# Graph attention on one core: comparison constants read from SBUF instead of PSUM, and self loops added by 8-column products

## The reference, cut to what matters

```
scores = einsum('ehd,ehd->eh', ft[src], ft[dst]) / sqrt(13)
agg    = segment_sum(ft[src] * softmax_over_dst(scores), dst)     # attention
...
s = concatenate([src, arange(n)]);  d = concatenate([dst, arange(n)])   # self loops
out = segment_sum(h[s] * norm[:, None], d)                         # each convolution
```

## Time and profile before

| what | value |
|---|---|
| median of 3 runs | 3872.35 us (3868.58 to 3874.59) |
| profiled execution, its own time | 3876.97 us |
| its span in the profile | 3875.2 us |
| busy share of the span: PE, DVE, ACT, POOL | 91%, 60%, 46%, 61% |
| mean granted clock of TensorE | 0.901 |

### The profile page before, as it was taken

One profiled execution on the slowest core, in us unless ns is written; L12 is line 12 of the kernel. 1 busy time (PEld: TensorE's weight loads), 2 busy tenths in 40 slices (PEclk: granted clock), 3 DMA queues, 4 the chain that ended last, 5 costly groups with the idle time before them and its releaser, 6 DMA issues. The chain is left out here.

```text
span 3875.2 us, 60488 instructions
## 1 busy us (share of the span) xinstructions
PE 3542.1 (91%) x21012; PEld 2105.9 (54%) x21012; DVE 2341.8 (60%) x3454; ACT 1786.6 (46%) x4890; POOL 2357.4 (61%) x2508
## 2 busy tenths in 40 slices
PE   5799999999999999999875888999999999999999
PEld 4566666666666666666654554444544454445444
DVE  8798888888888888888743674222322242214222
ACT  4788888878778878888621464000200020002000
POOL 2577777777777777777774001775277437734772
PEclk7688888888888888888876898999999999999999
DMA  6443334334343343333323215887788678868885
GB/s 203 123 109 105 106 103 107 106 104 106 106 107 103 107 106 103 107 107 107 99 64 78 49 35 163 257 256 223 220 258 256 203 238 258 257 193 261 261 261 176
DMA packets 494657, 599.82 MB, mean 155 GB/s; under 512 B 59929, under 2 KB 426868, under 8 KB 494094
## 3 DMA queue, kind: packets, MB, share of 16 engines
q1 hardware_dynamic: 358950, 341.00, 29.2%
q0 software_dynamic: 79888, 166.31, 17.6%
q10 hardware_dynamic: 55544, 89.04, 6.6%
HBM read 488.04 MB, written 109.69 MB: 154 GB/s over the span
## 5 line engine op out<-in xcount | busy, mean ns | idle before, releaser
L923 POOL DMA_INDIRECT fts<-ft_tab,src_all x1568 | 1481.1, 945 | 477.6 <-issue 477.3
L2296 PE MATMUL cv_acc<-cv_cnt,cv_parts 128*128 128x512 bf16 (+1 forms) x6468 | 1304.7, 364 | 1.0 <-DVE cv_y L2130 1.0
L2296 PEld LDWEIGHTS cv_acc<-cv_cnt,cv_parts 128*128 128x128 bf16 x6468 | 608.3, 98 | 693.4 <-DVE cv_y L2130 1.8
L2069 POOL DMA_INDIRECT cv_slots<-hs_tab,slot_idx x600 | 568.4, 947 | 416.4 <-issue 374.0
L960 DVE TENSOR_TENSOR ohk<-iota_ps,key_cols 128x784 bf16<-128x784 f32 x720 | 665.7, 966 | 5.6
L1212 PE MATMUL agg_ps<-terms,oh 128*64 128x141 f32 x2744 | 544.9, 372 | 35.9 <-DVE terms L997 35.3
L1053 ACT ACTIVATE dist_l<-lo_iota,low 128x128 bf16<-128x128 f16 x1800 | 545.2, 387 | 17.1 <-ACT low L1048 0.7
L1212 PEld LDWEIGHTS agg_ps<-terms,oh 128*64 128x64 f32 x2744 | 472.1, 185 | 90.8 <-DVE terms L997 76.3
L1105 ACT CAST strip<-adj_ps 128x392 bf16<-128x392 f32 x720 | 341.8, 475 | 256.2 <-PE adj_ps L1156 230.1
L974 DVE TENSOR_TENSOR prod<-ftd_ps,fts 128x780 f32<-128x780 f32 (+1 forms) x392 | 271.1, 692 | 285.3 <-DMA fts<-ft_tab,src_all 275.8
L2069 POOL DMA_INDIRECT spare<-hs_tab,slot_idx x296 | 280.2, 947 | 187.4 <-issue 187.4
(11 more groups left out here) (287 smaller groups left out, 3349.8 us busy)
## 6 DMA issues: line engine op xcount, KB each, us to landing
cv_cnt<-adj SPq DMA_DIRECT2D x88, 2048.0 KB, 8.5
cv_cnt<-adj SPq DMA_DIRECT2D x44, 2176.0 KB, 9.6
adj<-strip ACTq DMA_DIRECT2D x180, 392.0 KB
fts<-ft_tab,src_all POOLq DMA_INDIRECT x1568
win<-ft_tab SPq DMA_DIRECT2D x196, 65.0 KB
hs_tab<-cv_hs ACTq DMA_DIRECT2D x24, 448.0 KB, 3.8
cv_slots<-hs_tab,slot_idx POOLq DMA_INDIRECT x600
agg_tab<-res SPq DMA_DIRECT2D x196, 35.2 KB
```

The lines of the kernel that those rows point to most:

```text
L923: nc.gpsimd.indirect_dma_start(fts[u][:, k, :], None, ft_tab[:, :], bass.IndirectOffsetOnAxis(src_all[:, n, k:k + 1], 0)).then_inc(gathere ...
L2069: nc.gpsimd.indirect_dma_start(slots[n % RING][:, e, :], None, hs_tab[:, :], bass.IndirectOffsetOnAxis(slot_idx[:, k, at:at + 1], 0)).then ...
L2296: last = nc.tensor.matmul(a[:, 0:width], parts[:, r, b, :], cnt[q][:, 0:width // SUB, (b - b0) * SUB:(b - b0 + 1) * SUB], start=(b == 0 an ...
```

## The change

It has two parts. The first takes the iota bank away: `iota_ps` and the copy that filled it are gone, and lines 955 and 960 read both inputs, iota and keys, from SBUF. The second takes `own` and `own_low` away, with their two memsets and two copies and the semaphore `own_made` that TensorE waited on once at the start. Each quarter's first count product now opens the bank, and the self loops come last: one product of 8 columns, with the identity `ident_bf` (128 x 128, bf16) as weights and 8 of its columns as the moving operand, written to the 8 places of the quarter (2 of `a`, 4 of `d`) that are the strip's own nodes. The number of one-hot instructions, of gathers and of count products is the same as before.

```
-        own = sb("own", [SUB, NA, 2 * KEYS], BF16, c)
-        own_low = sb("own_low", [SUB, 2 * P - SUB], BF16, c)
-        iota_ps = pb("iota_ps", [P, 512], F32, c)
-        own_made = sem("own_made")
...
-            nc.vector.memset(own[:], 0.0).then_inc(own_made, 1)
-            nc.vector.memset(own_low[:], 0.0).then_inc(own_made, 1)
-            dve.wait_ge(own_made, 2)
-            nc.vector.tensor_copy(own[:, :, KEYS:KEYS + HALF], ident_bf[0:SUB, 0:SUB].rearrange("p (a d) -> p a d", d=HALF)
-                                  ).then_inc(own_made, 1)
-            nc.vector.tensor_copy(own_low[:, P - SUB:P], ident_bf[0:SUB, 0:SUB]).then_inc(own_made, 1)
...
             dve.wait_ge(iotas, 1)
-            nc.vector.tensor_copy(iota_ps[:, 0:KEYS + P], iota_sb[:]).then_inc(consts, 1)
-            dve.wait_ge(consts, 8)
-            key_no, lo_no = iota_ps[:, 0:KEYS], iota_ps[:, KEYS:KEYS + P]
+            dve.wait_ge(consts, 7)
+            key_no, lo_no = iota_sb[:, 0:KEYS], iota_sb[:, KEYS:KEYS + P]
...
-                tile_of = own[:, q * QS:(q + 1) * QS, KEYS - HALF * k.j:2 * KEYS - HALF * k.j]
-                nc.tensor.matmul(adj_ps[q % 2][:, 0:QS * KEYS], own_low[:, P - SUB - SUB * k.u:2 * P - SUB - SUB * k.u], tile_of, start=True, stop=False)
+                counts_ps = adj_ps[q % 2][:, 0:QS * KEYS]
                 for a in range(QS):
                     for m in range(SC):
                         n = q * QC + a * SC + m
-                        last = nc.tensor.matmul(adj_ps[q % 2][:, a * KEYS:(a + 1) * KEYS], ohl[:, k.s, n, :],
-                                                ohk[:, k.s, n, :], start=False, stop=(a == QS - 1 and m == SC - 1))
+                        nc.tensor.matmul(counts_ps[:, a * KEYS:(a + 1) * KEYS], ohl[:, k.s, n, :], ohk[:, k.s, n, :],
+                                         start=(a == 0 and m == 0), stop=False)
+                first = SUB * k.u + q * QS * HALF
+                last = nc.tensor.matmul(counts_ps.rearrange("p (a t d) -> p a t d", a=QS, d=HALF)[:, :, k.j, :], ident_bf[:],
+                                        ident_bf[:, first:first + QS * HALF].rearrange("p (a d) -> p a d", d=HALF),
+                                        start=False, stop=True)
                 last.then_inc(adj_done, 1)
...
             zero = Group(0)
-            pe.wait_ge(own_made, 4)
             nearness(zero)
```

## The result

The changed kernel takes 4075.99 us (median of 4 runs, 4065.62 to 4082.38) against 3873.47 (3868.58 to 3877.05) for the kernel before: a ratio of 1.0521, with an interval of 1.0496 to 1.0546. It is slower by 202.5 us, where +121 was predicted; the time lies inside the range, near its upper end.

The account below looks back on a forecast made before the run. The prediction took POOL's back-to-back gathers to bound the attention; 3877.0 us profiled plus 121 of gather waits made 3998, and the median lying 4.6 lower gave 3993 us, range 3918 to 4086.

Parts of the forecast that it names:

- What bounds the kernel: Attention: POOL issues gathers back to back, one every 1.249 us; 1568 of them make 1959 us, half the kernel.
- A gather waits at its start: Attention gathers: length is 0.94 us plus what was left of a VectorE instruction with two SBUF inputs, minus 0.12.
- rival 2: Attention: gathers are not held up, VectorE gives way within its idle time; time stays at 3872 us, chance 0.08.
- 0.74 x 0.49 + 0.26 x 1.19: Attention: short-kind and long-kind waits weighted by their shares before the change, 0.67 us a group, +121 us over 180 groups.
- long kind: Groups whose `prod` starts about 3.30 us after the eighth gather's start; fourth, seventh, eighth gathers wait, together 1.19 us.
- More than 0.1 us ahead: Attention: a gather waits only if the VectorE instruction with two SBUF inputs began more than 0.1 us before it.
- short kind: Groups whose `prod` starts about 2.60 us after the eighth gather's start; only the eighth gather waits, 0.49 us.
- Rival 1: Attention: a waiting gather cannot get in between gapless VectorE instructions; 1.87 us a group, +336, about 4208 us, chance 0.07.
- Rival 3: Whole kernel: the change frees time, by a few us of setup or quicker `ohk`; some 3865 us, chance 0.02.
- `ohk` at 975 ns: VectorE in the attention: 975 ns with both inputs in SBUF against 966 before, covered by idle time, so costing nothing.
- Self loops, clock, setup: TensorE some 0.7 us less a group beside the gathers, a lower clock, fewer setup instructions: none changes the time.

Follow-up runs that it names:

- the first experiment: Against the kernel before, only the iotas moved to SBUF, self loops left as they were: 4079.4 us, 1.0533 times the kernel before.
- the third: Against the kernel before, iotas read from SBUF, but each group's 22 keys first copied by VectorE into PSUM: 3872.2 us, 1.0003 times the kernel before.

## Why the prediction was right in kind and short in size

*What bounds the kernel*: right. The gaps stayed at 477.7 us, and the gathers' 197.8 us are 99% of what the span grew by.

*A gather waits at its start for a VectorE instruction with both inputs in SBUF, and goes on 0.12 us before its end*: right, taken from two gathers of another stage, and confirmed by the first experiment against the third, which differ in where the keys lie (and in the two small copies and waits that this takes). The Trainium skill, page "SBUF — State Buffer", section "Who interferes with whom", infers that `tensor_tensor` does not stall the making of descriptors. Taken for the whole gather, as in rival 2, the measurement decides against that, with 535 of 1568 delayed and 202.5 us; these gathers also read their indices from SBUF, and which of their steps is held no run here shows.

*The weights, "0.74 x 0.49 + 0.26 x 1.19"*: this is the step that mis-sized the sum. The shares of the two kinds were read from the kernel before and taken as fixed. They hang on the length of a group: it moves the last gather's end past the strip's store, so that 146 of 160 groups become long, a share of 0.91 and not 0.26. The long kind's walk, 1.19 us a group, would have given +214; measured are 11.09 - 9.99 = 1.10 us and +202.5. The range reached the measured time only because it took in this bound, and not as the likeliest. How near the walk comes is in part luck: the fourth, seventh and eighth gather wait 0.19, 0.33 and 0.47 us in the mean where it had 0.47, 0.21 and 0.51, and the other places add 0.11, which it had at nothing. That the store sets the kinds is shown by the two runs that move it; why a store delays the landing is not.

*"More than 0.1 us ahead"*: wrong for the fourth `ohk`, which has no wait in front of it. In the kernel after it cost a wait of 12 gathers only, since the long kind's third gather comes before `most`. But it makes the short kind's walk wrong: with the third gather held, the group takes 11.57 us (the store moved), 1.58 more than before and not 0.49. Had the shares stayed as they were, the sum would have been too low even so. With the wait in front of `ohk`, the short kind's eighth waits 0.5 us, as its walk said, and the seventh 0.1, which the walk had free.

*Rival 1*: out. A waiting gather gets in between `ohl` and `ohk` and between two `ohk`, as the 1.27 and the 1.47 show. *Rival 2*: out; `ohk` took 965 ns and the gathers gave way. *Rival 3*: out; the time rose.

*`ohk` at 975 ns*: 965, so the place of the iota makes no difference to VectorE, and the line through the earlier trace rows was 10 ns high. *Self loops, clock, setup*: nothing, as predicted; the run with the self loops alone has the lower clock and the time of before.

What stays open: why an instruction two places ahead of `ohk` (`most`, with a memset between) still counts. That instructions without a wait are handed on ahead of their start, and hold gathers from then on, fits all that was seen around the fourth `ohk`, the wait that releases the gathers above all; the handing itself is not in the trace. It does not fit the run of `ohl` and three `ohk` as it stands: the first `ohk` there has no wait in front either, and yet ten gathers that started in the last 0.14 us of `ohl`, up to 0.06 us ahead of that `ohk`, took 0.94 to 0.96 us. So the reach back has been seen behind `most` alone, and not behind another instruction with both inputs in SBUF.

## What to carry to other kernels

Before moving an operand from PSUM to SBUF, look at what GpSimd does in that stretch: where it issues indirect DMAs back to back, each VectorE instruction with both inputs in SBUF, if long like `ohl` and `ohk` here, can hold one of them up for about its own length, though it takes no longer itself. Weights that are counted in the kernel before (so many groups of one kind, so many of the other) are themselves an outcome of the timing; ask what sets them and work the sum out for each kind alone. Where such an instruction can't be had otherwise, a semaphore wait right in front of it gives gathers the time until it truly starts: with one instruction a group, behind `most`, the loss went from 98 to 27 us. In the kernel after, whose gathers mostly met other instructions, the same wait alone gave next to nothing (4071.0 us).

## What had not been expected of the hardware

- The hold can reach back beyond the start that the trace shows: gathers that started up to 0.37 us before the fourth `ohk` waited for it, when no semaphore wait stood in front of it, if `most` had started 0.05 us or more ahead of them. With a wait in front, they were held from about 0.1 us behind its start only.
- With a store of 392 KB from SBUF issued 0.3 to 1.3 us before a gather ends, its rows land some 0.6 us later (2.29 against 1.66 us in the mean from its end to `prod`, in the kernel before), which that kernel did not feel.
- The two inputs' place does not matter to VectorE's own time: an `ohk` takes 965 ns from SBUF and SBUF, 966 from PSUM and SBUF.
